# Order of TensorE's transposes and output sums in a two-lane state-space recurrence

## The reference, cut to what matters

```python
def step(h, inp):
    d_t, B_t, C_t, u_t = inp
    dA = jnp.exp(d_t[..., None] * A)
    h = dA * h + d_t[..., None] * B_t[:, None, :] * u_t[..., None]
    y_t = jnp.einsum('bdn,bn->bd', h, C_t)
    return (h, y_t)
...
_, ys = jax.lax.scan(step, h0, xs)
y = jnp.swapaxes(ys, 0, 1) + u * D_param
y = y * jax.nn.silu(res)
return y @ W_out
```

## Time and profile before

| | us |
|---|---|
| median of 3 runs | 1341.02 |
| lowest and highest | 1339.26, 1343.89 |
| the profiled execution's own time | 1337.38 |
| its span, from the first to the last instruction | 1335.7 |
| the two passes of the recurrence, each | 160.8 |

### The profile page before, as it was taken

One profiled execution on the slowest core, in us unless ns is written; L12 is line 12 of the kernel. 1 busy time (PEld: TensorE's weight loads), 2 busy tenths in 40 slices (PEclk: granted clock), 3 DMA queues, 4 the chain that ended last, 5 costly groups with the idle time before them and its releaser, 6 DMA issues. The chain is left out here.

```text
span 1335.7 us, 11403 instructions
## 1 busy us (share of the span) xinstructions
PE 909.3 (68%) x3350; PEld 481.4 (36%) x3352; DVE 909.8 (68%) x1735; ACT 613.4 (46%) x1697; POOL 282.8 (21%) x153
## 2 busy tenths in 40 slices
PE   3532746556899958989825155566569896898893
PEld 2421323222436523444414032222233563344342
DVE  1377555555649669999727874655564794899994
ACT  1305373442234447866721336533404342856882
POOL 1011035555315010000000100655531701000000
PEclk9755868888898879999956567888889796999997
DMA  7100022221000000000010002222200000000000
GB/s 200 28 0 1 5 87 94 71 71 55 0 0 1 1 0 0 1 1 1 0 45 0 1 0 67 74 89 74 71 8 1 0 1 0 0 1 1 0 1 16
DMA packets 31418, 35.74 MB, mean 27 GB/s; under 512 B 7684, under 2 KB 17658, under 8 KB 31354
## 3 DMA queue, kind: packets, MB, share of 16 engines
q1 hardware_dynamic: 29384, 33.02, 8.4%
q10 hardware_dynamic: 1970, 1.97, 0.5%
HBM read 33.67 MB, written 1.31 MB: 26 GB/s over the span
## 5 line engine op out<-in xcount | busy, mean ns | idle before, releaser
L1488 POOL TENSOR_TENSOR rs<-ve,minus_half 128x4 f32<-128x4 f32 (+2 forms) x60 | 102.0, 1708 | 819.6 <-DVE ve L1118 691.2
L728 PE MATMUL ps<-mem,ident 128*128 128x512 f32 x256 | 174.7, 820 | 121.5 <-POOL mem L1503 121.5
L876 PE MATMUL ps<-mem,ident 128*128 128x512 f32 x512 | 231.4, 600 | 30.6 <-DVE mem L1456 29.8
L1301 DVE TENSOR_TENSOR_SCAN mem<-mem,ps 128x1024 f32<-128x1024 f32 x64 | 146.3, 2287 | 139.1 <-PE ps L722 138.0
L1503 POOL TENSOR_TENSOR mem<-mem 128x1024 f32<-128x1024 f32 x64 | 177.2, 2769 | 216.5 <-DVE mem L1301 216.5
L1078 ACT ACTIVATE mem<-mem 128x32 f32<-128x32 f32 x1024 | 217.8, 311 | 0.0
L908 ACT ACTIVATE mem<-ps 77x512 f32<-77x512 f32 (+6 forms) x168 | 101.3, 605 | 249.8 <-PE ps L817 69.4
L1456 DVE SCALAR_TENSOR_TENSOR mem<-mem 128x1024 f32<-128x1024 f32 x128 | 159.4, 1282 | 13.4 <-ACT mem L1078 11.9
L994 ACT ACTIVATE mem<-mem,m_A 128x511 f32<-128x511 f32 x128 | 84.8, 712 | 151.3 <-DVE mem L1301 150.1
L876 PEld LDWEIGHTS ps<-mem,ident 128*128 128x128 f32 x512 | 93.9, 190 | 167.1 <-issue 92.7
L728 PEld LDWEIGHTS ps<-mem,ident 128*128 128x128 f32 x256 | 58.1, 252 | 196.2 <-POOL mem L1503 149.4
(11 more groups left out here) (220 smaller groups left out, 1253.5 us busy)
## 6 DMA issues: line engine op xcount, KB each, us to landing
mem<-bc_rows SPq DMA_DIRECT2D x96, 256.0 KB, 3.4
x<-in_x_dram SPq DMA_DIRECT2D x4, 256.0 KB, 3.5
out_dram<-x SPq DMA_DIRECT2D x4, 256.0 KB, 2.3
mask<-in_mask_BxSxS_ik_dram SPq DMA_DIRECT2D x4, 154.0 KB, 3.2
mem<-n_L_ffn_expert_down_dram SPq DMA_DIRECT2D x1, 512.0 KB
mem<-in_L_xattn_Wo_dram SPq DMA_DIRECT2D x1, 512.0 KB
mem<-in_L_xattn_Wv_dram ACTq DMA_DIRECT2D x1, 512.0 KB
a_q<-in_L_xattn_Wq_dram SPq DMA_DIRECT2D x1, 512.0 KB, 4.9
```

What stands on the lines that cost most here:

```text
L728: mm = pe.matmul(ps[:, j, :], ident[:], HC[s][:, n % 2, j, :], start=(n == 0), stop=(n == NS - 1), skip_group_check=True)
L876: mm = pe.matmul(ps[:, j, :], ident[:], WH[s][:, h % WB, j * 512:(j + 1) * 512], start=(h == 0), stop=(h == PH - 1), skip_group_check=True)
L1301: nc.vector.tensor_tensor_scan((HS, TU)[n % 2][s][:].rearrange(flat), dA[s][:, n % 2].rearrange(flat), dbu.rearrange(flat), 0.0, ALU.mult, ...
L1488: nc.gpsimd.tensor_tensor(RS[s][0:rows, i * n:(i + 1) * n], VE[s][0:rows, i * n:(i + 1) * n], minus_half[0:rows, 0:n], ALU.pow)\
```

## The change

On PE, the loop over the states runs one turn more, and the sum of state n-1 stands behind the transposes of state n in the same turn. The stage of the sum of state m goes from 4.5 + m to 4.8 + m, and so behind the transposes of state m+1 (4.7 + m) for both lanes. The last piece (the product with W_out) is moved from stage 5 + NS to 6 + NS, still behind all sums. No other engine's program is touched.

```diff
-                    for n in range(NS):
-                        if s in BLEND_LANES:
+                    for n in range(NS + 1):
+                        if n < NS and s in BLEND_LANES:
                             yield 3.7 + n
                             w.next(G("dz_ready", s))
                             if n == 0:
...
                             mm.then_inc(G("dbu_done", s), 1)
-                        yield 4.5 + n
-                        w.next(G("hc_done", s))
-                        for j in range(DJ):
-                            mm = pe.matmul(ps[:, j, :], ident[:], HC[s][:, n % 2, j, :],
-                                           start=(n == 0), stop=(n == NS - 1), skip_group_check=True)
-                        mm.then_inc(G("y_acc", s), 1)
-                    yield 5 + NS
+                        if n >= 1:
+                            yield 3.8 + n
+                            w.next(G("hc_done", s))
+                            for j in range(DJ):
+                                mm = pe.matmul(ps[:, j, :], ident[:], HC[s][:, (n - 1) % 2, j, :],
+                                               start=(n == 1), stop=(n == NS), skip_group_check=True)
+                            mm.then_inc(G("y_acc", s), 1)
+                    yield 6 + NS
```

## The result

| | before | after |
|---|---|---|
| median of the runs, us | 1342.42 (4 runs) | 1210.59 (4 runs) |
| lowest and highest | 1339.26, 1343.89 | 1207.60, 1212.48 |
| span of the profiled execution | 1335.7 | 1209.1 |
| one pass, end of first scan1 to end of last | 151.59 | 87.42 |
| one state in the middle | 10.24 | 5.84 |

The ratio is 0.902 with a 95% interval of 0.899 to 0.905. The forecast was 1215 us, 1205 to 1235.

What follows compares the result with a forecast made beforehand. A ring of waits through DVE's scan, POOL's product and PE's sum and transposes bounds it. Per pass (10.11 - 5.96) x 15 = 62.2 plus 0.6; two passes 125.6: 1341.0 - 125.6 = 1215 us, range 1205 to 1235.

Steps and rivals of the forecast that it cites:

- (a): PE's transposes for lane 1's scan no longer queue behind the output sum awaiting POOL; the scan's whole 4.51 us wait falls.
- (b): The recurrence's next bound: POOL's two products plus DVE's excluding product TT0, 5.96 us per state, above DVE's own 5.64.
- The hand-over: When POOL's product h0 ends, DVE's waiting TT0 takes the shared port before POOL's h1; TT0 grows to about 1.4 us.
- Rival 1: POOL's second product goes before DVE's TT0 at the shared port: state 8.3 us, time 1286 us, chance 0.06.
- (c): PE in the recurrence stays at the high clock: 4.80 us per state, 80% of 5.96, two gaps of about 0.6 us.
- Rival 2: PE's clock falls in the small gaps: 1241 us if half low, chance 0.10; 1300 us if always low, 0.03.
- (d): ACT's 4.1 us per state and the B and C transfers, at about 117 GB/s, stay hidden; cost 0.
- rival 3: Transfers of the B row land so late (22 us) that the state is 10.67 us: 1358 us, chance 0.01.
- rival 4: Lane 1's scan still waits, for ACT's product or exponential: a gain of anything down to zero, chance 0.02.
- (e): Ends of each pass: start loss booked 0, up to 1.8 us; lane 1's final step starts at 4.9 not 5.43, gaining 0.6.

Runs made afterwards that it cites:

- filler run: Kernel before, order untouched, with four more zero-weight matmuls behind each sum of lane 0 to fill PE's idle time: 1294.7 us, ratio 0.965.
- e_tt2: Changed kernel with DVE's product of lane 0 (TT0) done for the first of two blocks only, from state 2 on: 1187.0 us, ratio 0.885.
- last variant: Changed kernel with lane 0's scaled product made by PE in states 3, 5, ... 15, PE turning it ahead of y1(n-2), ACT's input one state earlier: 1189.3 us, 0.887.
- first variant: Changed kernel with lane 0's scaled product made by ACT and PE instead of DVE in states 3, 5, ... 15: 1203.2 us, again 1203.7 us.

## Why the prediction was right

What goes was right in mechanism and size. What bounds the new state came out near the measured time by a sum that names the wrong path, and that is in part luck.

- *What goes (a).* The 4.51 us wait was to fall entirely, and it did: 3.4 us are left in a pass, in the first state, where about 4 were forecast. The two runs that move one sum each show that y1 is the one that mattered. The prediction named y1 and h1 as what d1 stood behind; that lane 0's sum did not have to move it did not say.
- *What is late next (b).* POOL's state was forecast as 2.34 + 0.20 + 2.34 + 1.08 = 5.96 us, above DVE's 5.64. The state is 5.84, and DVE alone is 5.62. The terms 2.34 for h0 and 1.08 for TT0 behind it were right. The other two stand for the wrong thing. The 0.20 was read as a pause of POOL between two products; already in the earlier trace rows it is the wait for scan0 (h0 starts at 310.35, and scan0 ends at 307.98 + 2.29 = 310.27), and h1 begins without one. And h1 doesn't run its full 2.34 behind TT0: in the earlier trace rows it ends at 306.90 + 3.24 = 310.14, 2.19 behind TT0's end at 307.95, and in the new state 2.21 behind. So POOL is done first, and what the next h0 waits for is scan0, 2.40 us behind TT0's end. The forecast had h1 and the pause, 2.54, in that place. That these are within 0.14 of each other is luck; with a shorter h1 the same sum would have come out too low, since scan0 would stay. The 0.12 us a state make 3.6 us in two passes, most of the difference between 1215 and 1210.6.
- *The hand-over.* TT0 came first each time: it is 1.42 or 1.43 us long in 14 of the 16 states of each pass (all but the first two), as forecast (about 1.4). Rival 1 (POOL first, TT0 of 3 us or more) did not happen. The reason given against it, that POOL needs 0.20 us between two products, is not the one: h1's record begins where h0's ends, and TT0 still got its turn. What the runs show is that TT0, issued 0.3 us before h0 ended, went first.
- *The clock (c).* 1.00 in the middle of the pass, with PE busy 49.23 of 60 us (82%; forecast 80%) and gaps of 0.40 and 0.67 us a state. Rival 2 did not happen. The filler run confirms that the idle time had brought the clock down before.
- *Other engines (d).* Landing of B stayed at a median of 3.5 us, with 115 GB/s in the pass (117 forecast), and rival 3 did not happen. ACT's product was in time, so rival 4 did not happen either.
- *Both ends (e).* No loss at the start: d1(1) ran at the low clock (1.94 us), and the clock was up before d1(2) (1.04 us), ahead of its scan. The end came as worked out: lane 1's L1308 starts at 280.58, 4.90 us behind the last scan's end (271.21 + 4.47 = 275.68), where 4.9 was forecast and 5.43 was before.

```profile
188.40 1.94 PE L722 MATMUL ps<-ident,mem 128*128 128x128 f32 x8 [2.47 <-DVE mem L1302]
...
195.11 1.04 PE L722 MATMUL ps<-ident,mem 128*128 128x128 f32 x8
...
271.21 4.47 DVE L1302 TENSOR_TENSOR_SCAN mem<-mem,ps 128x1024 f32<-128x1024 f32 x2
278.00 1.41 DVE L1308 SCALAR_TENSOR_TENSOR mem<-mem,m_D,ps 128x512 f32<-128x512 f32 x2 [2.32 <-PE ps L729]
...
280.58 1.40 DVE L1308 SCALAR_TENSOR_TENSOR mem<-mem,m_D,ps 128x512 f32<-128x512 f32 x2
```

The account of the profiled executions: two passes 2 x (151.59 - 87.42) = 128.3 us less. The stretch ahead of the first pass is 2.3 us longer, the one between the passes (337.54 to 832.19 before, 275.68 to 772.45 after) 2.1 longer, the one behind the second 2.7 shorter, each with its pass end's 0.5 in it. Together 126.6, the difference of the spans. The forecast of 125.6 from the recurrence was 2.9% short of 129.4 (128.3 and twice 0.53).

## What to carry to other kernels

On an engine that works in program order, look in each ring of waits for what merely stands ahead: a step that feeds the next round belongs ahead of a step that only collects results, as soon as the collecting step waits for a slower engine. Then add up, per round, what each engine does alone. The largest sum is a lower bound, here DVE's 5.62 us and not the 4.8 of the engine that was edited. Then look for the next ring of waits, with the time for which one engine holds up another counted in. It can be longer than any engine's own sum: here it goes through two engines and takes 5.84. The sign of it here was a short wait that returned in each round on an engine that looked full. And where an engine idles for microseconds in each round, ask how much of its next step is slow because of that: here filling the idle time alone was worth 3.5%.

## What the runs showed of the hardware that was not expected

- The time that POOL loses beside a DVE product of two SBUF inputs is a little shorter than the time for which it has to wait: h1 is 0.98 us longer than 2.35, where TT0 runs 1.08 us behind h0. Before the change it started 0.16 us behind TT0, of 1.21, and lost 0.9. With a TT0 of 512 elements per partition (e_tt2), POOL's pair of products takes 5.12 instead of 5.64, 0.44 above 2 x 2.34.
- When TT0 and a second POOL product both stood behind a running POOL product, and TT0 had been issued first, it went first in all 28 cases of the changed kernel's profile, though POOL's two products follow each other without a pause.
- The stretch between the passes, whose instructions are the same in all these kernels, was 494.7 us before, 496.8 after, 493.7 when the changed kernel ran again and 488.6 in the kernel with the short TT0 (757.01 - 268.45). Between 100 and 150 us behind the first pass the granted clock was 0.76 in the first two and 0.83 in the third; the windows of the changed kernel in its two profiled executions:

```profile
375.68:425.68 50.00, 36.36 (x160) 21.41 (x159) 31.24 (x79) 15.08 (x25) 4.47 (x4) 0.76 0.00 1
```

```profile
377.79:427.79 50.00, 36.43 (x168) 21.45 (x167) 32.62 (x92) 16.61 (x28) 4.46 (x4) 0.83 0.00 1
```

  So one kernel's own executions differ by some microseconds in stages that the edit does not touch, with a clock that differs. The kernel with the short TT0 gained 7.8 us more than its passes give; it also hands other values to the stages behind. The last variant's median is 14.4 us under that of the first variant, where the passes give 7.1; but its profile is of its slowest execution (1200.1; the others took 1188.5 to 1194.5), where that stretch took 498.8 us, so no profile shows where the fast ones save. In the kernel with the short TT0 the clock of the same 50 us was 0.83 too, with 5.1 us less in the stretch than in the rerun, so the clock of this window isn't the whole cause. What is was not tried and stays open.
